# A four-layer graph network on one core: the second layer's messages summed with one-hot matrices 256 wide, and a scalar compare in the counting pass

## The chip, the core and the metric

The kernel runs on one core of a Trainium2 chip, as one launch. The metric is the device time of the launch in microseconds. The core has a matrix engine (TensorE, PE in the rows; PEld is its weight load), VectorE (DVE), ScalarE (ACT), GpSimd (POOL), which issues the gathers here, and SyncE (SP), which issues most plain transfers. Each has its own instruction queue, and they meet through semaphores. Matrix products go to PSUM, eight banks of 512 fp32 per partition.

## What is computed

3125 nodes with 128 features and 50000 edges, sorted by destination, go through four graph layers, each followed by a sum with its input and a layer norm:

```python
# layer 0, four steps: m = emb @ W_msg.T + b, one row per node and edge type
r = segment_sum(m[src, etype], dst); emb = gru(r, emb)
# layer 1
pe = relu(edge_attr_2 @ pos_w1) @ pos_w2
msg = pe * x[src] + x[src]
agg = segment_sum(msg, dst) / max(count(dst), 1)
out = relu(batchnorm(concat([x, agg]) @ sage_w + sage_b)) + x
# layer 2
messages = segment_sum(x[src] @ W_msg.T + b + embed[etype9], dst); out = gru(messages, x)
# layer 3: attention over the edges (softmax by destination), gate, graph norm, FFN
```

## The kernel before, in words

**Slots and waves.** The edges lie in 391 tiles of 128, an edge per partition. A tile is a slot, and a slot's messages are summed by one product: stationary the gathered rows (128 edges by 128 features, fp32), moving a one-hot matrix with a row per edge and a column per destination of a window, added into PSUM at the window's column. PSUM holds the sums for all 3200 padded nodes in banks 0 to 6. A tile that crosses a window's border needs a second slot. With windows of 128 nodes there are 24 such extra slots, padded to 416 (`SLOTS`), 52 waves of eight (`WAVES`); with windows of 256 (`PAIR`) there are 12, 403 slots (`P_SLOTS`), 51 waves (`P_WAVES`), the last with three (`P_LAST`). `cols` and `cols2` hold each slot's window column for the two widths, `dl` and `dl2` each edge's place in its window.

**Passes.** There are seven passes over all slots: four of the first layer (k = 0 to 3), the second layer's (`PASS_L1`), the third's (`PASS_L2`) and the fourth's (`PASS_L3`). Before the change the passes of the first and third layer use the 256-wide form, the second's and fourth's the 128-wide one (`single(k)`). In each, GpSimd issues one indirect gather per slot (L498), with each wave's eight into one of four ring buffers, and waits (`credit`) until TensorE has finished the wave of four before. `gat[u]` counts landings, `oh_ready` finished one-hot matrices. Between passes the sums are copied out (`evac`, L940 on VectorE and L561 on ScalarE) and the node update and norm run; the next table must be stored before the next pass's gathers start.

**One-hot matrices.** `pair_hot` (L904) makes a 256-wide one with a `tensor_scalar` per slot: an fp32 ramp of 256 compared with a scalar per partition from `dl2`. `one_hot` (L912) makes two 128-wide ones with a `tensor_tensor` of the ramp and a broadcast of `dl`, four per wave.

**The counting pass** is the first layer's last. Beside the message sum it counts the edges of each node by type: for every slot VectorE makes a second, bf16 one-hot matrix of 256 (L929, a `tensor_tensor` of the bf16 ramp `iotab` with a broadcast of `dlb`), and TensorE multiplies its two halves by a one-hot matrix of the type (L925) into bank 7.

**The second layer's pass** makes its messages on the way, a half wave (four slots) at a time, all through PSUM bank 7: TensorE's four hidden products (`wpad`, `rts`), ScalarE's ReLU (L619), TensorE's four position products (`pw`, `wt`), and VectorE's multiply with the gathered rows (L1083, 1 + pe times x, in place in the ring). TensorE puts four scatter products of the half wave before between hidden products and position products. At a turn's end (four waves) the last half's scatter is issued by itself (the lines after the `for u` loop), and the next turn starts with hidden products. VectorE makes the next wave's one-hot matrices (after a copy into `rts`, L1077) between the multiply of the first half and that of the second. Every product is issued from a helper (L1366), and a product in fp32 shows as two MATMUL instructions, so "x8" is four products.

Of the kernel before, what the change touches and what calls it, by code (L numbers as in the profile page):

```python
# [19 lines left out]
BF16 = mybir.dt.bfloat16  # L20
# [4 lines left out]
ds = bass.ds  # L25
# [71 lines left out]
def single(k):  # L97

    return isinstance(k, int) and k in (PASS_L1, PASS_L3)


def first_wave(k):

    if isinstance(k, int) and k > PASS_L1:
        return STEPS * P_WAVES + WAVES + (P_WAVES if k > PASS_L2 else 0) + (WAVES if k > PASS_L3 else 0)
    return k * P_WAVES
# [8 lines left out]
def landed(k, s, i):  # L115

    if isinstance(k, int) and k >= PASS_L1:
        whole = len(range(s, WAVES, RING)) * 16 * WV if s < RING else 0
        before = STEPS * pair_landed(s) + (whole if k > PASS_L1 else 0) + (pair_landed(s) if k > PASS_L2 else 0)
    else:  # L120
        before = k * pair_landed(s)
# [12 lines left out]
def build(nc, a, out, seen, known):  # L134
    ctx = ExitStack()
    with ctx:
# [23 lines left out]
        dl2 = sb("dl2", [P, P_SLOTS])  # L160
        dlb = sb("dlb", [P, P_SLOTS], BF16)
# [202 lines left out]
        def pair_turns(eng, body):  # L364
# [164 lines left out]
        def _(act):  # L529
# [84 lines left out]
            with act.Fori(0, TURNS) as i:  # L614
                for u in range(RING):
                    for hf in range(2):
                        q = (i * RING + u) * 2 + hf
                        act.wait_ge(l1_hid, q + 1)
                        nc.scalar.activation(pw[:, hf, :], ps[:, 7, :], ACT.Relu).then_inc(l1_relu, 1)  # L619
            evac(PASS_L1)  # L620
# [114 lines left out]
        def _(dve):  # L735
# [155 lines left out]
            step("i_oddf", V.tensor_copy(dl2[:, :], base_i))  # L891
            after("i_oddf")
            step("i_dl2", V.tensor_tensor(dl2[:, :], dl2[:, :], dl[:, 0:P_SLOTS], ALU.add))
            after("i_dl2")
            step("i_dlb", V.tensor_copy(dlb[:, :], dl2[:, :]))
# [21 lines left out]
            def sums(k, counting=False):  # L917
                bufs = 2 if counting else OH_BUFS

                def wave(i, u, n):  # L920
# [3 lines left out]
                    if counting:  # L924
# [145 lines left out]
            V.tensor_tensor(oh[:, 0, :, :], iota.unsqueeze(1).to_broadcast([P, WV, P]),  # L1070
                            dl[:, 0:WV].unsqueeze(2).to_broadcast([P, WV, P]), ALU.is_equal).then_inc(oh_ready, 1)
            with dve.Fori(0, TURNS) as i:
# [768 lines left out]
```

## Time and profile before

| | us |
|---|---|
| median of 3 runs | 4488.1 (4474.8 to 4493.0) |
| profiled execution, its time | 4481.7 |
| profiled execution, its span | 4480.0 |
| mean granted TensorE clock | 0.791 |
| TensorE busy | 2911.3 (65%) |
| VectorE busy | 1834.4 (41%) |
| GpSimd busy | 2757.7 (62%) |

Times in the trace count from the start of the span. A row of the timeline gives start, length, engine, line, operation, tiles and, in brackets, how long the engine had been idle before and what ended that. A row by stretches gives its bounds, its length, the busy time and (x) instructions of each engine, the granted clock, the DMA share and GB/s. A row of one line of the program gives the duration in ns (min/median/max) and the first and the last start. The granted clock is a share of 2.4 GHz; the engine runs at 1.2 or at 2.4 GHz, so 0.75 is half the time at each. The last multiplies of a pass and the copying out of its sums mark its end; its first gather marks the start.

### The profile page before, as it was taken

How to read it: one execution, taken by the hardware profiler on the slowest of the kernel's cores; microseconds unless marked ns; L12 is line 12 of the kernel's file. 1: busy time of each engine (PE TensorE's matmuls, PEld its weight loads, DVE VectorE, ACT ScalarE, POOL GpSimd, SP SyncE). 2: the span in 40 equal slices, each digit the busy share in tenths (PEclk: the TensorE clock that was granted, in tenths of full speed). 3: DMA queues.
4: the chain of work that ended last, by engine and by line, in shares of the span. 5: the costliest groups of instructions: out<-in, count | busy, mean ns of one | idle time of the engine just before them, and what ended most of it. 6: DMA issues, size and time to landing. Idle time of an engine off the chain costs nothing. (4 is left out here: it accounts for less than half of the span.)

```text
span 4480.0 us, 45699 instructions
## 1 busy us (share of the span) xinstructions
PE 2911.3 (65%) x12266; PEld 2199.9 (49%) x12267; DVE 1834.4 (41%) x4634; ACT 423.4 (9%) x692; POOL 2757.7 (62%) x2879
## 2 busy tenths in 40 slices
PE   6656575555765557777776676675566766562687
PEld 3444444444444444545546666544444565562574
DVE  4222252222522226555552222322222666667764
ACT  2000020000200002000021111210000111110334
POOL 3777737777377773777737777467775377772000
PEclk9777787777977779666679989877777888886899
DMA  5222222222222222222212222122221255551340
GB/s 178 53 52 52 53 83 53 52 52 53 83 53 52 52 52 83 52 51 51 51 36 52 52 52 52 30 55 53 52 53 38 89 155 155 155 156 51 113 131 15
DMA packets 144279, 314.17 MB, mean 70 GB/s; under 512 B 50083, under 2 KB 64618, under 8 KB 143706
## 3 DMA queue, kind: packets, MB, share of 16 engines
q0 software_dynamic: 97760, 214.03, 18.1%
q1 hardware_dynamic: 46458, 99.48, 6.4%
q8 instruction: 20, 0.33, 0.0%
q14 instruction: 41, 0.34, 0.0%
HBM read 251.68 MB, written 61.63 MB: 70 GB/s over the span
## 5 line engine op out<-in xcount | busy, mean ns | idle before, releaser
L498 POOL DMA_INDIRECT ring<-m_tab,idx x1612 | 1546.5, 959 | 720.5 <-issue 490.2
L1366 PE MATMUL ps<-oh,ring 128*128 128x256 f32 (+1 forms) x3694 | 1012.5, 436 | 485.2 <-DMA ring<-m_tab,idx 374.0
L1366 PE MATMUL ps<-nodes,ring 128*128 128x256 f32 x2000 | 765.2, 554 | 479.3 <-DMA ring<-m_tab,idx 378.1
L1366 PEld LDWEIGHTS ps<-oh,ring 128*128 128x128 f32 x3694 | 755.4, 248 | 628.7 <-issue 530.2
L498 POOL DMA_INDIRECT ring<-x_tab,idx x819 | 778.7, 951 | 261.5 <-issue 247.8
L1366 PEld LDWEIGHTS ps<-nodes,ring 128*128 128x128 f32 x2000 | 532.4, 282 | 618.4 <-issue 520.8
L904 DVE TENSOR_SCALAR oh<-iota,dl 128x256 f32<-128x256 f32 x1015 | 309.8, 375 | 932.1 <-PE ps L1366 931.7
L904 DVE TENSOR_SCALAR nodes<-iota,dl 128x256 f32<-128x256 f32 x1000 | 305.1, 375 | 832.5 <-PE ps L1366 832.5
L498 POOL DMA_INDIRECT ring<-kv_tab,idx x416 | 401.1, 964 | 149.2 <-issue 126.5
L508 POOL TENSOR_TENSOR small<-small,bc 128x4 f32<-128x4 f32 (+1 forms) x28 | 31.1, 1110 | 581.4 <-DVE small L1006 581.4
L1366 PE MATMUL ps<-wpad,rts 128*128 128x128 f32 x832 | 159.8, 371 | 199.5 <-DVE pw L1156 199.5
L1366 PE MATMUL ps<-nodes,wt 128*128 128x512 f32 (+1 forms) x532 | 231.3, 576 | 36.1 <-DVE nodes L940 11.2
L1366 PEld LDWEIGHTS ps<-wpad,rts 128*128 128x128 f32 x832 | 146.1, 272 | 211.6 <-DVE pw L1156 211.6
L561 ACT ACTIVATE nodes<-ps 128x512 f32<-128x512 f32 x18 | 9.4, 597 | 2507.8 <-PE ps L1366 2507.8
L912 DVE TENSOR_TENSOR oh<-cst,dl 128x256 f32<-128x256 f32 x624 | 223.7, 419 | 52.1 <-PE ps L1366 51.9
L1366 PE MATMUL ps<-rts,wpad 128*128 128x128 f32 x832 | 135.8, 312 | 151.3 <-DVE ring L1083 144.4
L1083 DVE SCALAR_TENSOR_TENSOR ring<-ps,ring 128x512 f32<-128x512 f32 x104 | 71.9, 692 | 382.5 <-DMA ring<-x_tab,idx 212.2
L1366 PEld LDWEIGHTS ps<-rts,wpad 128*128 128x128 f32 x832 | 114.0, 212 | 172.4 <-DVE ring L1083 162.5
L1366 PEld LDWEIGHTS ps<-nodes,wt 128*128 128x128 f32 x532 | 98.4, 197 | 158.1 <-issue 116.4
L1366 PEld LDWEIGHTS ps<-rec,pw 128*128 128x128 bf16 x806 | 105.4, 131 | 114.2 <-issue 66.9
L1155 DVE TENSOR_TENSOR ring<-ring,ps 128x512 f32<-128x512 f32 x104 | 71.1, 683 | 171.9 <-DMA ring<-kv_tab,idx 171.9
L929 DVE TENSOR_TENSOR pw<-iotab,dlb 128x256 bf16<-128x256 bf16 x403 | 139.2, 411 | 0.0
(247 smaller groups left out, 2496.5 us busy)
## 6 DMA issues: line engine op xcount, KB each, us to landing
ve_dr<-pw SPq DMA_DIRECT2D x52, 512.0 KB, 2.9
ring<-ve_dr SPq DMA_DIRECT2D x52, 512.0 KB, 3.4
ring<-m_tab,idx POOLq DMA_INDIRECT x1612, 2.5
m_tab<-ring SPq DMA_DIRECT2D x75, 256.0 KB, 2.2
ring<-x_tab,idx POOLq DMA_INDIRECT x819, 2.5
ring<-kv_tab,idx POOLq DMA_INDIRECT x416, 2.8
m_tab<-oh SPq DMA_DIRECT2D x25, 256.0 KB, 2.1
nodes<-in_xT SPq DMA_DIRECT2D x2, 1600.0 KB, 9.9
```

Of the source, the lines that this page charges most:

```text
L498: pool.indirect_dma_start(rows[:, j, :], None, table, bass.IndirectOffsetOnAxis(ap=idx[:, g * WV + j:g * WV + j + 1], axis=0)).then_inc(ga ...
L508: nc.gpsimd.tensor_tensor(rs[:, ws], sd[:, ws], b_("minus_half").to_broadcast([P, CH[c][1] // P]), ALU.pow).then_inc(ln_r, 1)
L561: nc.scalar.activation(gT[:, c0:c0 + cw], ps[:, c, 0:cw], ACT.Copy).then_inc(ev_a, 1)
L904: ins = V.tensor_scalar(pair_oh(u, j), iota2[:, :], dl2[:, ds((i * DEPTH + u) * WV + j, 1)], None, ALU.is_equal)
L912: ins = V.tensor_tensor(oh[:, v, j:j + 2, :], iota.unsqueeze(1).to_broadcast([P, 2, P]), dl[:, ds((i * RING + (u + ahead)) * WV + j, 2)].u ...
L929: ins = V.tensor_tensor(ohb2[:, u % 2, j, :], iotab[:, :], dlb[:, ds((i * DEPTH + u) * WV + j, 1)].to_broadcast([P, PAIR]), ALU.is_equal)
L1083: V.scalar_tensor_tensor(xj, ps[:, 7, :].rearrange("p (s d) -> p s d", d=D), 1.0, xj, ALU.add, ALU.mult).then_inc(l1_msg, 1)
L1155: V.tensor_tensor(kj, kj, pe_, ALU.add).then_inc(a_kv, 1)
L1366: return T.matmul(o, lhsT, rhs, start=start, stop=stop, skip_group_check=True)
```

## The change

The second layer's pass moves to the 256-wide form: 403 gathers in 51 waves, one-hot matrices from `pair_hot` in the buffers that the other such passes use, scatter products with 256 columns at `cols2`. Twelve turns run in the loop, three waves follow written out (`whole_turns`). The last wave gathers three slots, but its messages and products are made for eight; the five others have a place of -1 in `dl2` (it is longer now) and give all-zero one-hot rows. The hidden products, the ReLU, the position products and the multiply stay as they are. In the counting pass the bf16 matrices come from a `tensor_scalar` that compares the bf16 ramp with an fp32 scalar per partition from `dl2`, one for each slot as before, and `dlb` goes. Only the fourth layer's pass still has 128-wide matrices.

```diff
 def single(k):
-    return isinstance(k, int) and k in (PASS_L1, PASS_L3)
+    return isinstance(k, int) and k == PASS_L3
...
-        dl2 = sb("dl2", [P, P_SLOTS])
-        dlb = sb("dlb", [P, P_SLOTS], BF16)
+        dl2 = sb("dl2", [P, (P_WAVES + 1) * WV])
...
+        def whole_turns(eng, turn):
+            with eng.Fori(0, P_TURNS) as i:
+                turn(i, DEPTH)
+            turn(P_TURNS, P_REST)
...
+            step("i_dlz", V.memset(dl2[:, P_SLOTS:], -1.0))
-            step("i_dlb", V.tensor_copy(dlb[:, :], dl2[:, :]))
...
                         for j in range(n):
-                            ins = V.tensor_tensor(ohb2[:, u % 2, j, :], iotab[:, :],
-                                                  dlb[:, ds((i * DEPTH + u) * WV + j, 1)].to_broadcast([P, PAIR]),
-                                                  ALU.is_equal)
+                            ins = V.tensor_scalar(ohb2[:, u % 2, j, :], iotab[:, :],
+                                                  dl2[:, ds((i * DEPTH + u) * WV + j, 1)], None, ALU.is_equal)
...
-                            one_hot(PASS_L1, i, u, ahead=1).then_inc(oh_ready, 1)
+                            pair_hot(PASS_L1, i, u + 1, WV).then_inc(oh_ready, 1)
...
-                    last, cs = (cs if u else None), load_cols(pe, cols, i, u)
+                    last, cs = cs, load_cols(pe, cols2, i, u, turn=DEPTH)
...
-                                ins = mm(psf[:, ds(c0[4 * h0 + j], P)], ring[:, u0, 4 * h0 + j, 0:D],
-                                         oh[:, u0 % 2, 4 * h0 + j, :], start=False, stop=False)
+                                ins = mm(psf[:, ds(c0[4 * h0 + j], PAIR)], ring[:, u0, 4 * h0 + j, 0:D],
+                                         pair_oh(u0, 4 * h0 + j), start=False, stop=False)
...
-                    ins = mm(psf[:, ds(cs[4 + j], P)], ring[:, RING - 1, 4 + j, 0:D],
-                             oh[:, (RING - 1) % 2, 4 + j, :], start=False, stop=False)
+                    ins = mm(psf[:, ds(cs[4 + j], PAIR)], ring[:, waves - 1, 4 + j, 0:D],
+                             pair_oh(waves - 1, 4 + j), start=False, stop=False)
```

## Rows read from the trace of the kernel before

**Rows 1.** The page's chain that ended last, by engine
```profile
POOL 26%; issue 9%; PE 8%; DVE 3%; DMA 1%; ACT 1%; DVEq 0%; ACTq 0%
```

**Rows 2.** That chain inside the second layer's pass, by engine and line
```profile
by line: POOL ring L498 69.8%; issue 22.7%; PE ps L1366 5.5%; DVE ring L1083 1.1%; DMA ring<-x_tab,idx 1.0%; ACT pw L619 0.2%; DVEq L1081 0.0%
```

**Rows 3.** Busy time by stretch: second layer, third layer, counting pass, plain pass
```profile
2340.00:2852.00 512.00, 344.56 (x2411) 319.73 (x2410) 144.78 (x354) 59.71 (x100) 387.93 (x408) 0.90 0.20 52
2960.00:3430.00 470.00, 275.41 (x771) 211.28 (x770) 116.47 (x384) 0.00 (x0) 355.69 (x376) 0.75 0.21 53
1780.00:2240.00 460.00, 337.12 (x1426) 230.52 (x1427) 242.61 (x763) 0.00 (x0) 350.26 (x360) 0.67 0.20 51
1240.00:1660.00 420.00, 248.79 (x672) 189.99 (x671) 101.83 (x336) 0.00 (x0) 317.88 (x336) 0.73 0.20 52
```

**Rows 4.** Gather line by stretch: duration ns min/median/max, first and last start
```profile
L498 POOL DMA_INDIRECT ring<-x_tab,idx x416: 941/947/1210, 2335.7 to 2858.2; - x139
...
DMA to landing us min/median/max: 2.4/2.5/3.0
...
L498 POOL DMA_INDIRECT ring<-x_tab,idx x403: 940/946/1061, 2934.6 to 3438.0; - x135
...
L498 POOL DMA_INDIRECT ring<-m_tab,idx x360: 941/947/1117, 1780.3 to 2239.7; - x180
...
L498 POOL DMA_INDIRECT ring<-m_tab,idx x362: 940/947/1079, 1239.4 to 1692.1; - x181
```

**Rows 5.** Timeline, one wave of the counting pass, DVE and GpSimd: start, length
```profile
1856.09 2.75 DVE L929 TENSOR_TENSOR pw<-iotab,dlb 128x256 bf16<-128x256 bf16 x8
...
1856.88 1.11 POOL L498 DMA_INDIRECT ring<-m_tab,idx  x1 [0.30 <-issue]
...
1858.30 1.03 POOL L498 DMA_INDIRECT ring<-m_tab,idx  x1 [0.30 <-issue]
```

**Rows 6.** Timeline, one wave of a plain pass of the first layer
```profile
1436.68 2.55 DVE L904 TENSOR_SCALAR nodes<-iota,dl 128x256 f32<-128x256 f32 x8 [7.72 <-PE ps L1366]
1437.65 0.94 POOL L498 DMA_INDIRECT ring<-m_tab,idx  x1 [0.31 <-issue]
1438.90 0.95 POOL L498 DMA_INDIRECT ring<-m_tab,idx  x1 [0.30 <-issue]
```

**Rows 7.** Timeline, second layer's pass: end of a turn and the half waves after
```profile
2502.98 0.69 DVE L1083 SCALAR_TENSOR_TENSOR ring<-ps,ring 128x512 f32<-128x512 f32 x1 [2.80 <-PE ps L1366]
...
2508.53 0.69 DVE L1083 SCALAR_TENSOR_TENSOR ring<-ps,ring 128x512 f32<-128x512 f32 x1 [4.86 <-PE ps L1366]
...
2509.27 1.42 DVE L912 TENSOR_TENSOR oh<-cst,dl 128x256 f32<-128x256 f32 x4
...
2509.27 1.16 PE L1366 MATMUL ps<-rts,wpad 128*128 128x128 f32 x8 [0.79 <-DVE ring L1083]
...
2510.27 1.06 PE L1366 MATMUL ps<-oh,ring 128*128 128x128 f32 x8
2510.47 0.60 ACT L619 ACTIVATE pw<-ps 128x512 f32<-128x512 f32 x1 [3.19 <-PE ps L1366]
...
2511.16 1.11 PE L1366 MATMUL ps<-wt,pw 128*128 128x128 f32 x8
...
2512.31 0.69 DVE L1083 SCALAR_TENSOR_TENSOR ring<-ps,ring 128x512 f32<-128x512 f32 x1 [1.62 <-PE ps L1366]
```

**Rows 8.** Timeline, third layer's pass, its last three slots on TensorE
```profile
3443.11 1.46 PE L1366 MATMUL ps<-oh,ring 128*128 128x256 f32 x6
```

**Rows 9.** Timeline, end of the second layer's pass
```profile
2864.64 0.69 DVE L1083 SCALAR_TENSOR_TENSOR ring<-ps,ring 128x512 f32<-128x512 f32 x1 [1.62 <-PE ps L1366]
...
2866.65 2.08 DVE L940 COPY nodes<-ps 128x512 f32<-128x512 f32 x4 [1.32 <-PE ps L1366]
```

**Rows 10.** Timeline, second layer's pass, TensorE after a wait for a landing
```profile
2579.98 2.08 PE L1366 MATMUL ps<-rts,wpad 128*128 128x128 f32 x8 [3.24 <-DVE ring L1083]
```

**Rows 11.** The page's costliest groups, the one of the fp32 compare with a scalar
```profile
L904 DVE TENSOR_SCALAR oh<-iota,dl 128x256 f32<-128x256 f32 x1015 | 309.8, 375 | 932.1 <-PE ps L1366 931.7
```

More of the change, by code:

```diff
@@ L97, in single @@
 def single(k):
-    return isinstance(k, int) and k in (PASS_L1, PASS_L3)
+    return isinstance(k, int) and k == PASS_L3
 def first_wave(k):
-    if isinstance(k, int) and k > PASS_L1:
-        return STEPS * P_WAVES + WAVES + (P_WAVES if k > PASS_L2 else 0) + (WAVES if k > PASS_L3 else 0)
+    if isinstance(k, int) and k > PASS_L3:
+        return PASS_L3 * P_WAVES + WAVES
     return k * P_WAVES
@@ L115, in landed @@
 def landed(k, s, i):
[L117 to L121, printed above, removed]
+    before = k * pair_landed(s)
     if isinstance(i, int) and not single(k) and i * DEPTH + s == P_WAVES - 1:
@@ L611, in _, with relus @@
                 norm(0, c - 2)
-            with act.Fori(0, TURNS) as i:
-                for u in range(RING):
+            def relus(i, waves):
+                for u in range(waves):
                     for hf in range(2):
-                        q = (i * RING + u) * 2 + hf
+                        q = (i * DEPTH + u) * 2 + hf
                         act.wait_ge(l1_hid, q + 1)
                         nc.scalar.activation(pw[:, hf, :], ps[:, 7, :], ACT.Relu).then_inc(l1_relu, 1)
+            whole_turns(act, relus)
             evac(PASS_L1)
@@ L890, in _ @@
             after("i_odd")
-            step("i_oddf", V.tensor_copy(dl2[:, :], base_i))
+            step("i_oddf", V.tensor_copy(dl2[:, 0:P_SLOTS], base_i))
             after("i_oddf")
-            step("i_dl2", V.tensor_tensor(dl2[:, :], dl2[:, :], dl[:, 0:P_SLOTS], ALU.add))
+            step("i_dlz", V.memset(dl2[:, P_SLOTS:], -1.0))
+            step("i_dl2", V.tensor_tensor(dl2[:, 0:P_SLOTS], dl2[:, 0:P_SLOTS], dl[:, 0:P_SLOTS], ALU.add))
             after("i_dl2")
-            step("i_dlb", V.tensor_copy(dlb[:, :], dl2[:, :]))
             step("i_iob", V.tensor_copy(iotab[:, :], iota2[:, :]))
@@ L1069, in _, with messages @@
             V.tensor_scalar(rts[:, 0, :], recT[:, 0:P], 0.0, None, ALU.add)
-            V.tensor_tensor(oh[:, 0, :, :], iota.unsqueeze(1).to_broadcast([P, WV, P]),
-                            dl[:, 0:WV].unsqueeze(2).to_broadcast([P, WV, P]), ALU.is_equal).then_inc(oh_ready, 1)
-            with dve.Fori(0, TURNS) as i:
-                for u in range(RING):
+            pair_hot(PASS_L1, 0, 0, WV).then_inc(oh_ready, 1)
+            def messages(i, waves):
+                for u in range(waves):
                     for hf in range(2):
@@ L1548, in _, with messages @@
             zero(range(NCH))
-            with pe.Fori(0, TURNS) as i:
-                for u in range(RING):
-                    last, cs = (cs if u else None), load_cols(pe, cols, i, u)
+            def messages(i, waves):
+                cs = None
+                for u in range(waves):
+                    last, cs = cs, load_cols(pe, cols2, i, u, turn=DEPTH)
                     for hf in range(2):
-                        q = (i * RING + u) * 2 + hf
+                        q = (i * DEPTH + u) * 2 + hf
                         if hf == 0:
```

8 lines of the change are left out of this document (5 added, 3 removed).

## The prediction, made before the run

> **What bounds the kernel now.** I read the page's chain first: over the whole span GpSimd and its "issue" gaps are the largest entry, 26% and 9%, nearly all at the gather line [rows 1]. The chain inside the second layer's pass says the same of the stage that this change touches most: 69.8% gathers and 22.7% issue, 92.5% together, TensorE 5.5% [rows 2]. Then the table by stretches, for how near the other engines are: in the second layer's pass TensorE is busy 344.6 of 512 us at a granted clock of 0.90, in the third layer's pass, which already has the 256-wide matrices, 275.4 of 470 us at 0.75, in the counting pass 337.1 of 460 us at 0.67 [rows 3]. So a pass lasts as long as its gathers, and two numbers set it: how many, and at what pace.
>
> The paces come from first and last gather start [rows 4]: second layer 415 intervals in 522.5 us, 1.2590 us; third layer 402 in 503.4, 1.2522; counting pass 359 in 459.4, 1.2797; a plain message pass of the first layer 361 in 452.7, 1.2540. The instructions are the same; the passes differ by what VectorE does beside them. In the counting pass the two gathers that start while the eight bf16 compares run (tensor against broadcast tensor) take 1.11 and 1.03 us, not the median 0.95; before each GpSimd waits for nothing but 0.30 us of its own issue [rows 5]. In a plain pass the gathers under eight fp32 compares with a scalar per partition take 0.94 and 0.95 [rows 6]. I read that as: the two-tensor compare holds gathers up, the scalar one hardly does.
>
> **The change, part by part.**
>
> *Gathers and turns of the second layer.* 416 gathers become 403, 415 intervals become 402. The two-tensor compares (four per wave of two slots each) become eight scalar ones, so the pace should be that of the passes that have those: 1.2522 to 1.2540 us. 402 of these are 503.4 to 504.1 us against 522.5: a gain of 18.4 to 19.1, taken as 18.8. If the pace stayed 1.2590, the pass would be 506.1 and the gain 16.4.
>
> *VectorE in that pass.* One wave's compares go from 1.42 us [rows 7] to about 2.55 [rows 6]. They run after the first half's multiply, while TensorE works toward the second; multiply 0.69, copy and compares end about 3.4 us after its start, and the next multiply is due 3.8 us after it now and later than that with the change. Cost 0. Without this cover it would be 1.1 us for each of 51 waves, 58 us.
>
> *TensorE in that pass, the real cost.* A half wave is a closed chain, since everything goes through one PSUM bank: multiply on VectorE, four hidden products, four scatter products (ReLU of 0.60 us beside them), four position products, next multiply. At the higher clock (2.4 GHz) it repeats in 3.79 us, 2508.53 to 2512.31, and over the end of a turn in 5.55, 2502.98 to 2508.53 [rows 7]. A turn of four waves is 7 x 3.79 + 5.55 = 32.1 us, against 32 gathers in 40.3: slack 8. Four scatter products 128 wide take 0.89 us start to start (2510.27 to 2511.16); for 256 wide three take 1.46 with about 0.17 of tail [rows 8], so 0.43 each and 1.72 for four. That is 0.83 more for each half wave: 4.62, a turn of 38.7 us. The gathers of a turn then take 32 x 1.2522 to 1.2540 = 40.1. TensorE stays under them by 1.4 us a turn, 3.5%. Cost in the steady part 0; it is the thinnest cover here, and what it costs when gone is the first rival.
>
> *The end of the pass.* Here the longer chain shows. Now the last gather starts at 2858.2 [rows 4], lands 2.5 us later, and the banks are copied out from 2866.65 [rows 9]: 5.95 us after landing. With the change the last wave has only three gathers, so the wave before it lands just 3.75 us earlier, but both are still computed over eight slots. The wave before starts its first multiply about 3.3 us before the last landing (0.15 after its own landing, plus 0.3 of backlog from the turn's end three half waves before); then three half waves at 4.62, a multiply 0.69, a wait 0.13 and four last scatters 2.0: copying out begins 13.4 us after the last landing. Loss 7.5 us, up to 12 if TensorE is at 1.2 GHz for a stretch there.
>
> *Counting pass.* The 403 bf16 compares change form; matmuls, gathers and buffers stay, TensorE still waits for the landing of each wave. VectorE is idle for 217 of 460 us, 4.7 us in each of 46 waves [rows 3], so only the pace of the gathers matters. From 1.2797 to 1.2522 to 1.2540 us over 402 intervals: a gain of 10.3 to 11.1, taken as 10.7. No row shows a scalar compare in bf16. Below, the fp32 form bounds it (no delay). Above, the gain is 0 if the delay belongs to the work and not to the form, or it is a loss if the instruction holds GpSimd for its length (the second rival). I take the fp32 scalar compare, since it differs in type alone.
>
> The Trainium skill speaks against this. "SBUF — State Buffer", section "Who interferes with whom", lets a tensor_scalar in a two-port mode shut GpSimd out of the port pair for the whole instruction, while a tensor_tensor with two SBUF inputs takes only the read side, inferred there to leave the writing of descriptors alone. By that rule both edits would slow the gathers. The trace has it the other way round at its one comparable place [rows 5, 6]: 1.11 and 1.03 us under the tensor_tensor, 0.94 and 0.95 under the fp32 tensor_scalar. The bf16 case is open.
>
> *The rest.* One conversion of 403 elements at the start goes and a small memset comes; the first gathers wait for the table's store, not for these. The first matrices of the second layer's pass take about 1 us more on VectorE, before the first gather has landed. The turns become 12 and three waves written out, as in the other passes. Together 0.
>
> **Sum.** -18.8 + 7.5 - 10.7 = -22.0 us. On the profiled execution's 4481.7 us (span 4480.0 and 1.7 around it) that gives 4459.7. The median of the runs lies 6.4 higher, at 4488.1; the same difference gives 4466, and with some odds for a stretch at 1.2 GHz at the end I say 4467: 0.47% faster. About 0.5% (22 us) is what a measurement of this kernel can tell from no change, so this forecast sits on the edge of it.
>
> **Rivals.**
>
> *A: TensorE's chain becomes the bound.* The 38.7 us hold at 2.4 GHz. Of them 8 x (0.89 + 0.89 + 1.72) = 28 are matmuls, which take twice as long at 1.2 GHz, so a turn is 38.7 + 28y, with y the share of the work done at the lower clock. It decides at y = 0.05 (40.1). With the granted clock of now, 0.90, a fifth of the time is at 1.2 GHz, y = 0.11, a turn 41.8; 12.5 us for the first wave and 12.75 turns are 545 us from the first gather to the end of the chain, against 531 now and 520 by my forecast: 4493. At 0.86 it would be 4511, 0.5% slower; at the 0.75 of the third layer's pass about 4572. For it: the slack is 3.5%. Against it: the slow groups of this pass come after long waits for a landing, as at 2579.98 after 3.24 us of idling [rows 10], and in a closed chain with waits of 0.8 us the groups ran at 2.4 GHz [rows 7]. When TensorE is behind it has no long wait, so it should be fast exactly then; four waves of buffers carry a short slow stretch. Chance 0.13, of which 0.05 is beyond 0.5% slower. This is the one on the other side.
>
> *B: the scalar compare holds GpSimd for its length.* With one compare's 0.375 us [rows 11] for each of the two gathers of a wave that meet them, 0.75 in place of the 0.24 of now [rows 5], the counting pass would lose 51 x 0.51 = 26 us rather than gain 10.7: 4504; and if the compares of the second layer did so as well, another 51 x 0.75 = 38: 4542. For it only the rule above; against it [rows 6]. Chance 0.04.
>
> *C: the counting edit does nothing* (a wave needs both compares, and the start of TensorE's wave falls together with the slow gathers too): 4467 + 10.7 = 4478. Chance 0.09.
>
> *The forecast*: 0.72, its own range 4458 to 4474. Something not thought of: 0.02.
>
> **Numbers.** Within the forecast a little over half lies under 4465.7, 0.5% below 4488.1: faster 0.41. Slower is A's tail, B and a little else: 0.09. Same: 0.50. The range reaches below to both gains in full and a short end (4455) and above to A at the clock of now (4494).
>
> **What the profile after would show.** Second layer: 403 gathers in 503 to 505 us from first to last start, next to no waits for TensorE; half waves of 4.6 us; granted clock above 0.93; copying out 13 to 14 us after the last landing. Counting pass: 1.252 to 1.255 us from gather to gather, none of 1.11 under the bf16 compares. Wrong if: gathers of the second layer wait for TensorE's credit (A); gathers above 1 us stand under the compares with a scalar (B, C); or the end of the pass is much shorter than 13 us, which would make the gain larger than I say.

## The result

The kernel after takes 4451.9 us (median of five runs, 4450.7 to 4452.6) against 4485.3 of the kernel before beside it (4474.8 to 4493.0). The ratio is 0.9929, 95% interval [0.9918, 0.9939]: 33 us or 0.7% faster. I had forecast 4467, 0.47% faster, and a range down to 4455; the time lies 3 us below the range. A later set, on a chip where before had a median of 4485.7, gave 4454.7 and 0.9926 [0.9909, 0.9944]; that is 0.3 us below the range.

The two profiled executions differ by less: span 4450.7 against 4480.0. A second profile of the same kernel (run j1 below) has a span of 4465.3. So one execution can lie 15 us beside another, and I read every difference from both. Where they stand among their like matters below: the profiled execution of before took 4481.7 us, 3.6 less than the median; that of after took 4452.5, 0.6 more than its median; that of j1 took 4467.1, the slowest of its four (4450.5 to 4467.1).

The table by stretches of the kernel after, columns as in [rows 3]: second layer's, third layer's, counting, plain pass.

```profile
2340.00:2830.00 490.00, 377.60 (x2346) 334.31 (x2345) 189.01 (x534) 58.51 (x98) 371.16 (x391) 0.99 0.21 52
2960.00:3400.00 440.00, 260.19 (x704) 198.82 (x704) 106.66 (x352) 0.00 (x0) 332.74 (x353) 0.73 0.21 53
1780.00:2240.00 460.00, 300.15 (x1472) 208.40 (x1472) 194.63 (x772) 0.00 (x0) 347.96 (x368) 0.79 0.21 52
1240.00:1660.00 420.00, 247.73 (x670) 189.25 (x669) 101.32 (x336) 0.00 (x0) 317.75 (x336) 0.73 0.21 52
```

TensorE is busy for 377.6 of 490 us in the second layer's pass, 77% against 67% in [rows 3], and its granted clock rose from 0.90 to 0.99: with fewer waits it runs at 2.4 GHz nearly all the time. The gather line, whole passes, as in [rows 4]; second layer, third layer, counting pass:

```profile
L499 POOL DMA_INDIRECT ring<-x_tab,idx x403: 940/944/1085, 2325.9 to 2830.4; - x135
...
  PE ps L1370: 5.5, 18
...
L499 POOL DMA_INDIRECT ring<-x_tab,idx x403: 940/944/1073, 2909.2 to 3411.9; - x135
...
L499 POOL DMA_INDIRECT ring<-m_tab,idx x403: 940/944/2475, 1748.5 to 2253.4; - x135
```

403 gathers in 504.5 us, 18 of them released by TensorE after waits that are no longer than their own issue (5.5 us in 18). TensorE was behind for a while at the start of the pass, where its granted clock was 0.56 over the first 20 us (columns as before):

```profile
2325.90:2346.00 20.10, 12.29 (x50) 9.96 (x49) 3.75 (x11) 1.19 (x2) 15.22 (x17) 0.56 0.19 50
```

Wave 4's first multiply came 6.2 us after that wave's last gather, where 2.7 is usual. The buffers took that up, and by wave 8 it was 3.7 us. The chain of waits inside the second layer's pass, as in [rows 2]:

```profile
by line: POOL ring L499 46.3%; PE ps L1370 27.9%; issue 15.8%; DVE ring L1085 5.3%; DMA ring<-x_tab,idx 4.0%; ACT pw L620 0.7%; DVEq L1083 0.1%
```

Gathers and issue were 92.5% of it and are 62.1%; TensorE is now on it for 27.9%. I read that as TensorE's chain being as late as the gathers in such places; the gather line above shows that the gathers didn't wait for it. The end of the second layer's pass, by timeline, where [rows 9] has the old one:

```profile
2829.16 0.69 DVE L1085 SCALAR_TENSOR_TENSOR ring<-ps,ring 128x512 f32<-128x512 f32 x1 [4.46 <-DMA ring<-x_tab,idx]
...
2830.35 0.97 POOL L499 DMA_INDIRECT ring<-x_tab,idx  x1 [0.30 <-issue]
2830.90 1.89 PE L1370 MATMUL ps<-nodes,ring 128*128 128x256 f32 x8
...
2833.79 0.69 DVE L1085 SCALAR_TENSOR_TENSOR ring<-ps,ring 128x512 f32<-128x512 f32 x1 [1.57 <-PE ps L1370]
...
2838.48 0.69 DVE L1085 SCALAR_TENSOR_TENSOR ring<-ps,ring 128x512 f32<-128x512 f32 x1 [4.00 <-PE ps L1370]
...
2843.11 0.69 DVE L1085 SCALAR_TENSOR_TENSOR ring<-ps,ring 128x512 f32<-128x512 f32 x1 [1.71 <-PE ps L1370]
...
2845.96 2.08 DVE L942 COPY nodes<-ps 128x512 f32<-128x512 f32 x4 [2.16 <-PE ps L1370]
```

Three half waves of 4.63, 4.69 and 4.63 us follow one another after the last full wave has landed, and copying out begins 15.6 us after the last gather's start, 8.5 before.

Where the time went, by first and last start of the gather line and the start of copying out, in us:

| | before | after (difference) | j1, the same kernel (difference) |
|---|---|---|---|
| start to first gather | 58.5 | 56.4 (-2.1) | 57.7 (-0.8) |
| first three passes with node work | 1691.4 | 1692.1 (+0.7) | 1691.8 (+0.4) |
| counting pass, gathers | 516.6 | 505.0 (-11.6) | 507.9 (-8.7) |
| its tail and node work | 69.2 | 72.4 (+3.2) | 72.6 (+3.4) |
| second layer's pass, gathers | 522.5 | 504.5 (-18.0) | 505.9 (-16.6) |
| its tail (last gather to copying out) | 8.5 | 15.6 (+7.1) | 15.7 (+7.2) |
| node work behind it | 67.9 | 63.2 (-4.7) | 66.8 (-1.1) |
| third layer's pass, gathers | 503.4 | 502.7 (-0.7) | 503.7 (+0.3) |
| its tail and node work | 99.0 | 98.2 (-0.8) | 98.9 (-0.1) |
| fourth layer's pass, gathers | 526.7 | 524.1 (-2.6) | 524.8 (-1.9) |
| from there to the end | 416.3 | 416.6 (+0.3) | 419.5 (+3.2) |
| span | 4480.0 | 4450.7 (-29.3) | 4465.3 (-14.7) |

The three rows that the edits touch by my account sum to -22.5 and -18.1; I had -22.0. The rest is -6.8 in one execution and +3.4 in the other. Of the 18.0 us in the second layer's pass, 13 gathers fewer at 1.25 us are 16.3; the pace gives the small remainder.

### The profile page after: what moved, and what is told of

It reads as the page before. It is cut to its first block and busy times, and to the rows that moved or that the text cites. A ratio compares the mean times of both kernels' runs of the same rounds, so it can differ in the third digit from the quotient of the medians.

```text
span 4450.7 us, 45534 instructions
## 1 busy us (share of the span) xinstructions
PE 2896.7 (65%) x12218; PEld 2186.0 (49%) x12219; DVE 1826.0 (41%) x4838; ACT 421.9 (9%) x690; POOL 2727.8 (61%) x2866
## 5 line engine op out<-in xcount | busy, mean ns | idle before, releaser
L1370 PE MATMUL ps<-oh,ring 128*128 128x256 f32 (+1 forms) x3278 | 952.0, 454 | 482.9 <-DMA ring<-m_tab,idx 387.6
L1370 PE MATMUL ps<-nodes,ring 128*128 128x256 f32 x2400 | 849.5, 521 | 516.9 <-DMA ring<-m_tab,idx 404.1
L1370 PEld LDWEIGHTS ps<-oh,ring 128*128 128x128 f32 x3278 | 700.4, 243 | 632.6 <-issue 525.8
L1370 PEld LDWEIGHTS ps<-nodes,ring 128*128 128x128 f32 x2400 | 600.5, 265 | 666.0 <-issue 560.7
L499 POOL DMA_INDIRECT ring<-x_tab,idx x806 | 764.1, 948 | 255.5 <-issue 239.2
L907 DVE TENSOR_SCALAR oh<-iota,dl 128x256 f32<-128x256 f32 x1223 | 370.4, 374 | 933.1 <-PE ps L1370 932.7
L907 DVE TENSOR_SCALAR nodes<-iota,dl 128x256 f32<-128x256 f32 x1208 | 367.8, 375 | 871.1 <-PE ps L1370 871.1
L1370 PE MATMUL ps<-rts,wpad 128*128 128x128 f32 x816 | 118.9, 290 | 102.0 <-DVE ring L1085 102.0
L915 DVE TENSOR_TENSOR oh<-cst,dl 128x256 f32<-128x256 f32 x416 | 148.8, 420 | 51.7 <-PE ps L1370 51.7
L1370 PE MATMUL ps<-nodes,rec 128*128 x832 | 122.5, 311 | 0.0
```

The lines of the kernel that those rows point to most:

```text
L499: pool.indirect_dma_start(rows[:, j, :], None, table, bass.IndirectOffsetOnAxis(ap=idx[:, g * WV + j:g * WV + j + 1], axis=0)).then_inc(ga ...
L907: ins = V.tensor_scalar(pair_oh(u, j), iota2[:, :], dl2[:, ds((i * DEPTH + u) * WV + j, 1)], None, ALU.is_equal)
L915: ins = V.tensor_tensor(oh[:, v, j:j + 2, :], iota.unsqueeze(1).to_broadcast([P, 2, P]), dl[:, ds((i * RING + (u + ahead)) * WV + j, 2)].u ...
L1370: return T.matmul(o, lhsT, rhs, start=start, stop=stop, skip_group_check=True)
```

## The experiments

Eighteen kernels ran, on four chips. On chip 8 (the four runs j) the kernel before took 4485.7 us. On chips 6, 10 and 5 the same program had medians of 5150.2 to 5171.5, and no execution under 5127. What differs there is shown under "Two kinds of chips"; ratios are only compared on the same chip.

### The kernel after again, and its chain lighter, heavier and shorter (chip 8)

**j1**: the kernel after, unchanged.

> The kernel after once more. If a wave's work begins 2.7 us after its last gather again, the total is near 4452 us, 0.993 of before, with 504 us of gathers in the second layer's pass. If it begins 30 us after, the total is near 5168 us and equals before within 0.4%, with 660 to 680 us in that pass against 648 to 664 before, as the chain of multiply and products is then never idle for a landing. Node work behind that pass: 63 to 64 us where the granted clock there is 0.76 or more, 66 to 68 where it is 0.68; a third value would speak against the clock as its cause.

Measured 4454.7 us, 0.9926 [0.9909, 0.9944]. Its row of the gather line for the second layer's pass, which stands beside the first of the fence above:

```profile
L499 POOL DMA_INDIRECT ring<-x_tab,idx x403: 943/947/1098, 2330.0 to 2835.9; - x135
```

The median gather is 3 ns longer (947 against 944), and gathers that start while VectorE does nothing follow each other in 1.2509 us against 1.2482 (counted over the timeline's rows). The profile of before has 1.2502, j2 and j3 1.2514, j4 1.2488. So this pace belongs to the execution and not to the kernel; over the 2800 gathers of seven passes 2.7 ns would be 7.6 us, about half of what separates the two profiles of this kernel; the seven gather rows of the table differ by 6.7 in all.

The node work behind the pass by stretches, columns as in [rows 3]; before, after and j1:

```profile
2866.65:2934.60 67.95, 50.13 (x179) 32.29 (x179) 29.70 (x68) 21.27 (x35) 8.17 (x8) 0.67 0.08 25
```
```profile
2845.90:2909.20 63.30, 44.71 (x176) 28.23 (x175) 29.67 (x68) 20.60 (x34) 8.18 (x8) 0.76 0.09 27
```
```profile
2851.60:2918.40 66.80, 47.12 (x172) 30.33 (x173) 29.44 (x68) 20.66 (x34) 8.15 (x7) 0.69 0.08 25
```

VectorE's busy time is nearly the same in all three, TensorE's is 50.1, 44.7 and 47.1 us at a granted clock of 0.67, 0.76 and 0.69, and the stretch takes 68.0, 63.3 and 66.8. Over all profiles the kernels with the second layer's edit lie between 63.2 and 66.8 us there (14 profiles, mean 65.1), those without it between 65.9 and 67.9 (six, mean 67.2). So the expectation's two values were too neat. At 0.76 and more the stretch took 63.2 to 63.6 us, at 0.71 64.4 and 65.3, at 0.67 to 0.69 anything from 64.8 to 67.9: the time goes with the clock roughly, and at the same clock it still varies by 3 us. With the edit the node work behind its pass is some 2 us shorter in the mean.

**j2 and h1**: scatter products of 128 columns instead of 256, so the upper half of each pair's window is left out.

```diff
-    ins = mm(psf[:, ds(c0[4 * h0 + j], PAIR)], ring[:, u0, 4 * h0 + j, 0:D],
-             pair_oh(u0, 4 * h0 + j), start=False, stop=False)
+    ins = mm(psf[:, ds(c0[4 * h0 + j], P)], ring[:, u0, 4 * h0 + j, 0:D],
+             pair_oh(u0, 4 * h0 + j)[:, 0:P], start=False, stop=False)
```

> The kernel after with 128 columns in each scatter product of the second layer's pass (the upper half of each window pair is left out). With prompt landings: gathers 504 us as before, tail 15.6 to about 12.3 us, 3 to 4 us faster than after. With late ones: the first look gave 678.6 us of gathers for this kernel and 678.8 for after; if the length of the products has no part in it the two are again within 10 us of each other and only the tail is shorter, by 3 to 7 us; if it has, this one is 20 us or more shorter.

Measured on chip 8: 4448.6 us, 0.9915 [0.9899, 0.9932]; gathers 505.9 us, exactly j1's, tail 12.5 against 15.7 (3.2 shorter). So the wide products cost nothing while gathers run, and 3.2 us at the end. The clock of the pass goes back to 0.90: with the narrow products TensorE has waits again, and that width is all that differs.

**j3 and h2**: one more product for each half wave.

```diff
                         pe.wait_ge(l1_relu, q + 1)
+                        mm(ps[:, 6, 256:512], w("L3_Wskip"), iota2[:, :], start=False, stop=False)
```

> The kernel after with one more product for each half wave, 42.1 us of chain a turn. With prompt landings: first gather to copying out about 550 us or more, total 25 to 35 us above after (rival A's slack of 1.4 us a turn is real); gathers at 504 would mean that the slack is larger than I worked out. With late ones the first look gave 781.8 us, 103 more than after, 8 us for each turn where the product itself is worth 3.4 us: again 760 to 800 if that is the mechanism's and not one execution's.

Measured on chip 8: 4464.4 us, 0.9948 [0.9931, 0.9965], 9.7 us above j1 and not 25 to 35. No gather waited for TensorE, and yet the slack was overdrawn. Gather line and the end of the pass:

```profile
L499 POOL DMA_INDIRECT ring<-x_tab,idx x403: 943/947/1074, 2326.5 to 2829.8; - x135
its engine sat idle before it (us, times) until:
  issue: 122.6, 402
  DMA x_tab<-ring: 5.3, 1
```
```profile
2847.68 0.69 DVE L1085 SCALAR_TENSOR_TENSOR ring<-ps,ring 128x512 f32<-128x512 f32 x1 [4.43 <-PE ps L1370]
...
2852.74 0.69 DVE L1085 SCALAR_TENSOR_TENSOR ring<-ps,ring 128x512 f32<-128x512 f32 x1 [2.13 <-PE ps L1370]
2855.59 2.09 DVE L942 COPY nodes<-ps 128x512 f32<-128x512 f32 x4 [2.16 <-PE ps L1370]
```

The tail is 25.8 us, 10.1 more than j1's. From a wave's last gather to its first multiply it takes 5.8 us at wave 4, 6.3 at wave 8, and so on by 0.5 for each turn up to 11.4 at wave 48 (first two starts read from the timeline). A turn of this chain is therefore 0.5 us over the 40.05 of its gathers, 40.55: seven half waves of 4.99 and one of 5.59. Without the product it is 7 x 4.57 + 5.6 = 37.6. I had 38.7 and 42.1. The half wave is 0.05 shorter than I worked out, and the half wave at the turn's end, 5.55 in [rows 7], stays 5.6 and hides the wider scatter. So the slack is 2.4 us a turn, not 1.4. The kernel after shows it by itself: from wave 4 to wave 8, one turn, it made up 2.4 us of its backlog (6.2 to 3.7), and j1 2.7 (6.4 to 3.7). Even past the bound the four buffers take the backlog up, and it is paid once, at the end. That holds while the backlog stays within the buffers, as here (at wave 48 it is 8.7 us over the usual 2.7, and a wave's gathers take 10).

**j4**: the empty second half of the last wave is left out, which changes no result.

```diff
+                        if isinstance(i, int) and u == waves - 1 and hf:
+                            continue
```

(the same on VectorE and ScalarE, and the last scatter is of three slots).

> The kernel after without the empty second half of the last wave of the second layer's pass (no messages, no products for slots that don't exist). With prompt landings the tail goes from 15.6 to about 11 us and the total is 4 to 5 us lower than after's. With late landings the tail is 4 to 7 us shorter (29.6 against 35.4 in the kernel that also had this edit). The node work behind it ends the sooner the higher the clock is: 63 to 64 us at 0.76 to 0.78. Rival: the saved half wave comes back as a slower clock in the node work (66 us), and nothing is gained.

Measured 4448.3 us, 0.9914 [0.9895, 0.9933]; tail 12.0 us. The tail is 3.7 us shorter, 6 us in the medians; the interval overlaps j1's. Of the versions that compute everything it has the lowest median, by a margin that these runs can't confirm.

### Each edit alone (chips 6, 10, 5)

> The counting edit alone, on the kernel before. My theory (the two-tensor compare holds gathers up, the scalar compare does not): first to last gather start of the counting pass 516.6 -> 505 us, the gathers under the bf16 compares back to a pace of 1.25 us, all other passes as before, total -11 us (ratio 0.9975). Rival 1 (the delay belongs to the second compare as work, not to its form): 516.6 stays, total within 2 us of before. Rival 2 (what the forecast missed, some 9 us, came with this edit, for instance by a faster pace of every gather): total -16 us or more.

> The counting edit alone, repeated. My theory: the counting pass's gathers 516.6 -> 505 us where landings are prompt, total -11 us. Rival 1 (the delay belongs to the work, not to the form): no change. Rival 2 (the part that the forecast missed came with this edit): -16 us or more.

> The kernel before with the counting pass's edit alone. If my terms hold: 10.7 us faster, ratio 0.9976. If the missing 10 us belong to this edit (the lower amount of delayed gathers, other clock behind it): 20 us faster, 0.9955. In the profile: 505 to 508 us of gathers in the counting pass against 516.6, second layer's pass as before (522.5, tail 8.5, node work 67.9). On a chip with late landings 0.997 to 0.9985 again.

The counting edit alone: 0.9985 [0.9971, 0.9998], 0.9965 [0.9938, 0.9993], 0.9973 [0.9945, 1.0001]: 9 to 14 us faster in the medians, each time, though the third interval just reaches 1. The gathers under the bf16 compares follow in 1.28 us against 1.40 in the profile of before on chip 6 (e3). The pass's own gathers take 585.8 us against 589.6 there, and 585.8 on chip 10 against 593.1 in the two kernels without this edit (f2, h3), and on chip 5 581.3 against 583.5 (k2): 2 to 7 us of the gain stand in its row.

> The second layer's pass in the 256-wide form alone, counting compare as before. My theory: gathers 522.5 -> 504 us, end of the pass 7 us longer (15.5 us from the last gather's start to the copying out instead of 8.5), and the node work behind the pass 4 to 5 us shorter than before's 67.9, since TensorE comes out of a closed chain at 2.4 GHz: total -15 to -16 us (ratio 0.9965). Rival (node work unchanged, the clock there was luck): total -11 us. Rival (the chain bounds the pass): gathers over 515 us.

> The second layer's edit alone, repeated. My theory where landings are prompt: gathers 522.5 -> 504 us, end 7 us longer, node work behind the pass some 4 us shorter than 67.9 at a higher granted clock: total -15 us. Rival (that node work was luck of the clock): -11 us.

> The kernel before with the second layer's edit alone. If my terms hold: 18.8 less 7.5 = 11.3 us faster, ratio 0.9975. If the node work behind the pass gains by the clock on top, as its time fell from 67.9 to 63.2 to 66.8 us in kernels with this edit: 13 to 16 us, 0.9965 to 0.997. If all the missing 10 us belong to it: 21 us, 0.9953. In the profile: 504 to 506 us of gathers, tail 15.6, half waves of 4.57 us. On a chip with late landings 1.003 again, with 660 to 670 us of gathers in this pass.

The second layer's edit alone: 1.0031 [1.0012, 1.0051], 1.0031 [1.0007, 1.0056], and on chip 5 0.9949 [0.9924, 0.9975]. Its own pass takes 666, 662 and 659 us of gathers where the kernels without it have 655 (e3), 664 (e1), 648 (f1), 674 (h3) and, on chip 5, 713 (k1). No sign can be given for this edit there, and the sum that I wanted to split on these runs stays unsplit.

> The kernel before, again, for its own spread: by the clock theory the gaps between passes differ from run to run by 1.5 to 5 us each with the granted clock in them, while gather times of each pass stay within 0.5 us (504, 506, 506, 517, 522.5, 503.4, 527). Rival (the pace of all gathers varies by run): the plain passes' gather times differ from the first profile by over 0.5 us in the same direction.

> The changed kernel again, beside the next three. On a chip where gathers land in 2.5 us as in the first profiles: ratio to before 0.993, gathers of the counting pass 505 and of the second layer's pass 504.5 us, 15.5 us from the last gather to the copying out. On a chip that holds landings back by 20 us every third wave, as the one of the first four experiments did, the passes are bound by those stalls and the heavier chain of the second layer's pass shows: ratio about 1.00.

Before against itself: 0.9998 [0.9974, 1.0022]. The kernel after: 1.0008 [0.9982, 1.0033]. The gain is not there on chip 10.

### The form of the compare

**e4**: the 256-wide matrices of the second layer's pass by a compare of two tensors.

```diff
-                    ins = V.tensor_scalar(..., dl2[:, ds(..., 1)], None, ALU.is_equal)
+                    ins = V.tensor_tensor(pair_oh(u, j), iota2[:, :],
+                                          dl2[:, ds((i * DEPTH + u) * WV + j, 1)].to_broadcast([P, PAIR]),
+                                          ALU.is_equal)
```

> The changed kernel, but the second layer's 256-wide matrices made by a two-tensor compare (eight a wave) instead of the compare with a scalar. If the form of the compare sets the delay: about two gathers per wave meet it at +0.12 us, the pass's gathers 504.5 -> 514 to 517 us, total +10 to +12 us against the changed kernel. If the form does not matter: 504.5 stays. By the Trainium skill's port rule (SBUF - State Buffer, Who interferes with whom) the two-tensor form should leave the gathers alone: 504.5 or less.

Measured 1.0052 [1.0033, 1.0072]. One wave of it on VectorE and GpSimd:

```profile
2667.38 2.76 DVE L914 TENSOR_TENSOR oh<-iota,dl 128x256 f32<-128x256 f32 x8
2668.46 1.17 POOL L499 DMA_INDIRECT ring<-x_tab,idx  x1 [0.30 <-issue]
2669.93 1.04 POOL L499 DMA_INDIRECT ring<-x_tab,idx  x1 [0.30 <-issue]
2671.27 0.94 POOL L499 DMA_INDIRECT ring<-x_tab,idx  x1 [0.30 <-issue]
```

**h3**: the kernel before with eight scalar compares 128 wide in that pass.

> The kernel before with one edit: the 128-wide one-hot matrices of the second layer's pass are made by eight compares with a scalar per partition, not four tensor-against-broadcast ones. 416 gathers, narrow scatter and the counting pass stay. Theory F (the form of the compare delays the gathers that start under it): the gathers under these compares go from 1.32 us to about 1.25 to 1.27 from start to start, and the pass loses up to 3 us (522.5 to 519.6) where landings are prompt; the total moves by 2 to 3 us, within what can be measured. Theory W (the width or the amount of data sets the delay): a little over 1.3 us stays. In the stalled state only the pace can be read, not the total.

Measured 1.0017 [0.9996, 1.0037]. Start to start of the gathers that start while compares run, over the whole pass and without those that a stall follows, with how many of them took over 1.3 us:

| compare in the second layer's pass | us | over 1.3 us |
|---|---|---|
| two tensors, 256 wide (e4) | 1.331 | 57 of 85 |
| two tensors, 128 wide (e3; before) | 1.323; 1.321 | 18 of 47; 16 of 51 |
| scalar, 128 wide (h3) | 1.281 | 33 of 77 |
| scalar, 256 wide (f0; k2) | 1.252; 1.267 | 3 of 95; 14 of 90 |
| scalar, 256 wide (after; j1) | 1.275; 1.281 | 23 of 99; 26 of 98 |

At 256 wide the form makes 0.05 to 0.08 us a gather. At 128 wide it makes 0.04, and the share of delayed gathers is about the same for both, so theory F is right for the form that this change introduces and weaker in general. A scalar compare isn't free either. The time of the whole pass doesn't show the form: e4's gathers take 669.5 us, between 666.4 (e2) and 678.8 (f0), all bound by the stalls.

The two forms also differ on VectorE's side. The compare lines, j1 (scalar) and e4 (two tensors), durations in ns min/median/max:

```profile
L907 DVE TENSOR_SCALAR nodes<-iota,dl x200: 333/347/553, 2342.3 to 2827.6; 128x256 f32<-128x256 f32 x100
...
L914 DVE TENSOR_TENSOR oh<-iota,dl x184: 409/413/468, 2667.4 to 3263.4; 128x256 f32<-128x256 f32 x184
```

Of j1's 394 scalar compares in the pass, 75 start 0.5 to 0.7 us after a gather's start; 71 of these, and no others, take about 0.54 us instead of 0.34. No two-tensor compare is lengthened like that. So with the scalar form it is mostly VectorE that waits beside a gather, with the two-tensor form it is the gather. VectorE has the room for it (its compares still end before the next multiply), while the gathers set the length of the pass where nothing stalls.

### More work or other work around the pass

**f3**: the kernel after with ten dummy products behind each of the last two full waves of every pass outside the second and fourth layer's.

```diff
+                    if isinstance(i, int) and u < P_REST - 1:
+                        for _ in range(10):
+                            mm(ps[:, 6, 256:512], w("L3_Wskip"), iota2[:, :], start=False, stop=False)
```

> The changed kernel with ten extra 128x128x256 fp32 products into an unused part of bank 6 behind the last two full waves of each pass of the first and third layer (their results are never read). Clock theory (what TensorE did at a pass's end sets the time of the node work behind it): last full wave at 2.4 GHz, so from the last gather to the copying out 3 us less in each of five passes, and the node work at a granted clock near 1.00 (52.1 us in the first layer, 60.9 or less after the counting pass instead of 64.3): total -10 to -15 us against the changed kernel. Rival (the clock of the node work is set inside it): node times as they are, total within 3 us or longer by the extra products.

Measured 1.0086 [1.0052, 1.012]. Tails of up to 22.9 us, node work of 53.7 to 54.0 in the first layer where f0 has 52.1 to 53.8, and 62.5 behind the counting pass as in f0 (62.6); only that behind the third layer's pass is shorter (89.8 against 91.5). The warming costs more than it brings.

> The kernel after, but each scatter product of the second layer's pass has 128 columns instead of 256 (it leaves out the upper half of each window pair, so its sums are not the reference's). 403 gathers stay, the chain of a half wave goes back from 4.69 us to about 3.8, a turn from 38.7 to about 32 of 40.1 us of gathers. Theory P (the wide scatter costs only at the end of the pass while landings are prompt, and becomes the bound once landings stall): where landings are prompt (kernel before near 4485 us) the gathers of this pass stay at 503 to 505 us and only the tail behind the last gather gets 3.3 us shorter (15.6 to about 12.3 us), so the kernel is 3 to 4 us faster than after. Where landings stall (kernel before near 5150 us) the gathers of this pass fall from 679 us to 630 to 655 and the kernel is 25 to 45 us faster than after. Theory Q (in the stalled state the pass is slow by its number of stalls, whatever the chain): 679 us stay.

Measured 0.9992 [0.9967, 1.0017] on chip 10, 678.6 us of gathers against 678.8 in f0: theory P falls, theory Q stands. Half the columns change nothing in that pass.

> The kernel after with one more product of 128x128x256 in fp32 for every half wave of the second layer's pass, into an unused part of a bank; a turn of TensorE's chain goes from 38.7 to about 42.1 us, over the 40.1 us that its gathers take. Theory A (the chain is just under the bound, slack 1.4 us a turn): where landings are prompt the pass is now set by TensorE: from first gather to copying out about 12.5 + 12.75 x 42.1 + the rest = 550 us or more against 520 of after, gathers wait for TensorE, the kernel is 25 to 35 us slower than after. Where landings stall it is slower by 20 to 45 us too, since the chain catches up nothing. Theory Z (TensorE has much more room than the 1.4 us that I worked out): the gathers stay at 504 us and only the end grows, by about 1.5 us.

Measured 1.019 [1.0134, 1.0245], 781.8 us of gathers, 103 more than f0. All 103 are waits of GpSimd (280 us against 177); the gathers between them keep their pace. That a heavier chain costs 103 us and a lighter one brings nothing fits neither theory; I have none.

**h4**: j4's edit, and scalar compares in the fourth layer's pass too.

> The kernel after with two additions: the last wave of the second layer's pass, which has only three slots, makes no messages and products for its empty second half, and the fourth layer's pass makes its one-hot matrices with eight compares with a scalar per partition. The first should take one half wave of 4.6 us off the tail of the second layer's pass (15.6 to 11 us). The second should take away the slow gathers of the fourth layer's pass (36 of 47 under the compares are over 1.3 us, mean 1.39): 415 intervals from 1.263 to about 1.252 us, 524.1 to 519.5 us. Together 9 us faster than after where landings are prompt. Rival: the fourth pass's end hangs on other work and the 4.6 us there are not seen in the total. In the stalled state a gain under 10 us can hardly be told; the tail and the pace can.

Measured 1.0054 [1.0032, 1.0075]. The gathers of the fourth layer's pass take 695.6 us against 662.9 (f0), though those under the compares are quicker (1.29 against 1.37): GpSimd's waits in it grew from 138 to 174 us. This edit is a loss there and was not tried on chip 8.

### Two kinds of chips

On chips 6, 10 and 5 every pass is longer and the node work isn't (52.1 us in both). A plain pass of the kernel after on chip 10, by timeline. TensorE's products of the second row end at 1393.7, and none follow until the last row:

```profile
1386.64 2.45 DVE L907 TENSOR_SCALAR nodes<-iota,dl 128x256 f32<-128x256 f32 x8 [3.32 <-PE ps L1370]
...
1389.96 3.72 PE L1370 MATMUL ps<-nodes,ring 128*128 128x256 f32 x16
...
1412.57 2.53 DVE L907 TENSOR_SCALAR oh<-iota,dl 128x256 f32<-128x256 f32 x8 [23.48 <-remote]
1412.67 1.06 POOL L499 DMA_INDIRECT ring<-m_tab,idx  x1 [4.52 <-remote]
...
1415.23 5.45 PE L1370 MATMUL ps<-oh,ring 128*128 128x256 f32 x16 [21.56 <-issue]
```

VectorE waits 23.5 us and GpSimd 4.5, both until something that the profile doesn't know ("remote"), within 0.1 us of each other; it comes again 34.24 us later (1446.81), three waves of gathers on. The 16 such waits of GpSimd in a plain pass sum to 72 us, which is what the pass is longer. In the second layer's pass a wave's first multiply comes some 30 us after its last gather (median 30.9 in e3, 33.7 in f0) where it comes 2.7 us after it on chip 8 and in the two first profiles, and GpSimd waits at nearly every wave. Gathers between the stalls keep their 1.25 us. No run here tells what the stalls are; they are in before and after alike.

## Why the prediction was wrong, and where it was right

The mechanism was right. By its steps:

- *Gathers of the second layer*: forecast -18.8, measured -18.0 and -16.6. The pace was 1.2550 and 1.2585 us, not 1.2522 to 1.2540, since the scalar compares still delay about a quarter of the gathers that they meet (23 of 99 and 26 of 98).
- *VectorE in that pass*, cost 0: right. The compares of 2.3 to 2.6 us end before the next multiply.
- *TensorE in that pass*, cost 0 in the steady part: right, shown by j2, whose gathers take the same 505.9 us. The half wave is 4.57 us (forecast 4.62), the turn 37.6 (38.7), the slack 2.4 us (1.4).
- *The end of the pass*: copying out 13.1 us after the last landing (15.6 less 2.5), forecast 13.4; loss 7.1 and 7.2, forecast 7.5. Of it 3.2 are the wide products (j2) and 3.7 the empty half wave (j4).
- *Counting pass*: forecast -10.7, measured -11.6 and -8.7. One of my own signs of being wrong came all the same: gathers above 1 us do stand under the bf16 scalar compares (10 of 53 and 28 of 54 follow in over 1.3 us). Under the two-tensor ones it had been 93 of 99, and twice as many gathers met them, since the compares lasted longer.
- *The page that I set against it*: I took the rule of the Trainium skill ("SBUF — State Buffer", "Who interferes with whom") to make the scalar form the worse one for the gathers. No run agrees: the edit alone was 9 to 14 us faster three times, and e4's two-tensor compares delayed more gathers than any scalar one. But I had used half of the section: it also has a VectorE instruction with two SBUF inputs contending with a GpSimd instruction that reads SBUF (a gather here reads its indices from an SBUF tile), and in a two-port mode whichever comes first keeps the ports while the other waits. Both fit the rows under "The form of the compare", the second with VectorE as the one that mostly waits; that these compares run in such a mode no row says outright. Only the page's inference that the two-tensor form leaves the writing of descriptors alone has no support here.
- *Sum*: -22.0 forecast; -22.5 and -18.1 by the two profiles. That the first is so near is partly luck: undisturbed gathers followed in 1.2482 us in that execution and 1.2502 in the profile of before, and over 402 gathers in each of two passes these 2.0 ns are 1.6 us that belong to no edit (an estimate from the two paces).
- *Rivals*: A did not come, beyond a backlog over the first waves of the pass that the buffers took up. What I wrote against it held: the clock rose to 0.99 as the waits went. Its price was wrong as well: j3, 0.5 us a turn over the bound, lost 10 us at the end and none in the gathers. B and C are excluded for chip 8 by the counting pass's 505.0 and 507.9 us.

The step that failed is the last of the parts, "The rest ... Together 0", together with the carrying of one profile's sum to the median of the runs ("the same difference gives 4466"). The forecast was 15.1 us too high, and the first pair of profiles splits that:

| | forecast | measured | part of the miss |
|---|---|---|---|
| the terms of the sum | -22.0 | -22.5 | 0.5 |
| the rest | 0 | -6.8 | 6.8 |
| from the profiled execution to the median, with the odds for a slow end | +7.3 | -0.6 | 7.9 |

*The carrying.* I added 6.4 us because the profile of before lay that far below the median of three runs, and 0.9 more for the odds. With two more runs the median of before was 4485.3, so the distance was 3.6 and not 6.4. And it belonged to one execution of before: the profiled execution of after took 0.6 us more than its median, not 6.4 less. j1's profiled execution took 12.4 more than its own.

*The rest.* In the first pair, -4.3 of the -6.8 us are the gathers of the five passes that no edit touches (-0.2, -0.3, -0.5, -0.7, -2.6), about what 2.0 ns for each of their 2023 intervals make: the pace of that execution, not the change. The largest single row is node work. I said that TensorE is slow after long waits and fast without them, applied it to the pass, and stopped at its end, but the node work begins behind it: 4.7 and 1.1 us less in the two profiles at a clock of 0.76 and 0.69 against 0.67, some 2 us in the mean of all. The +3.2 and +3.4 behind the counting pass are not the edit's, as far as the profiles show: its node work takes 61.0 us at 0.84 or 64.3 at 0.79 in kernels of either kind (j3, with the edit, has 61.0; e3, the kernel before, 64.3).

What stays open: the medians gained 33 and 31 us, the terms explain 22.5 and 18.1. In the first set 4 us more are where the two profiled executions stood among the others, and the rest is the 6.8 above. In j1's set the rest is +3.4 and the profiled execution the slowest of four, so it can't serve as a check to within 10 us. How much of the gain beyond the terms comes from the edits was not separated: each edit would have to be timed alone on a chip like number 8, and the runs for that met chip 5.

## What to carry to other kernels

Where a ring of buffers lies between a steady producer and a chain, compare the chain's turn with the producer's, but as long as the backlog stays within the ring, price an overdraft as backlog per turn times turns, paid once at the end of the pass, and not as a new bound. When an edit fills the waits of TensorE, follow its clock into the stage behind, too. And before a difference of 0.5% is worked out from one profile, ask how far two profiles of one kernel lie apart (here 15 us, two thirds of the whole sum), and don't carry the place of one kernel's profile among its runs over to the other kernel.

## What the runs showed of the hardware

- TensorE's granted clock in the same pass went 0.90, 0.99, 0.90 as its scatter products were narrow, wide, narrow again (before, after, j2): nearly all the time at 2.4 GHz where half waves of 4.57 us left it few waits.
- The pace of undisturbed gathers is the same within 1 ns over the first six passes of an execution and differs between executions of one kernel: 1.2482 us (after) or 1.2509 (j1).
- Compares on VectorE delay gathers by their form, 256 wide: two tensors 1.33 us from start to start, a scalar 1.25 to 1.28, nothing beside them 1.25. Beside gathers 71 of 394 scalar compares took 0.54 us instead of 0.34 (j1); no two-tensor one did so (e4, at most 0.47).
- On three of four chips GpSimd stands still for some 4.5 us every 24 gathers of a plain pass, and VectorE waits some 23 us at the same points, at no extra time in node work: 5150 us against 4485 for one program. The cause is open.
